# A causal mask moved from VectorE's maximum to TensorE, with a new written-out order of the first pass

## What is computed

```python
h = _ln(x, ln1_g, ln1_b)
qkv = h @ W_attn + b_attn
q, k, v = jnp.split(qkv, 3, axis=-1)
...
att = jnp.einsum('bhtd,bhsd->bhts', q, k) * scale
causal = jnp.tril(jnp.ones((T, T), bool))
att = jnp.where(causal[None, None], att, -jnp.inf)
att = jax.nn.softmax(att, axis=-1)
sa = _merge(jnp.einsum('bhts,bhsd->bhtd', att, v)) @ W_aproj + b_aproj
x = x + sa
```

## Time and profile before

| | |
|---|---|
| median of 3 runs | 4394.42 us |
| lowest and highest | 4390.21, 4397.11 us |
| the profiled execution | 4394.35 us |
| its span, first to last instruction | 4392.4 us |
| busy over the span: TensorE matmul, VectorE, ScalarE, GpSimd | 97%, 84%, 58%, 34% |
| matmuls | 33536 |
| mean granted TensorE clock | 0.987 |

### The profile page before, as it was taken

One profiled execution on the slowest core, in us unless ns is written; L12 is line 12 of the kernel. 1 busy time (PEld: TensorE's weight loads), 2 busy tenths in 40 slices (PEclk: granted clock), 3 DMA queues, 4 the chain that ended last, 5 costly groups with the idle time before them and its releaser, 6 DMA issues. The chain is left out here.

```text
span 4392.4 us, 98493 instructions
## 1 busy us (share of the span) xinstructions
PE 4270.3 (97%) x33536; PEld 3443.1 (78%) x33536; DVE 3687.5 (84%) x12709; ACT 2543.8 (58%) x6753; POOL 1481.0 (34%) x1941
## 2 busy tenths in 40 slices
PE   5999999999999899999999999999999999999998
PEld 4788888888887678777787878778888888888886
DVE  4899999999997899999999999967777777777774
ACT  2556565665655454545555454536676767676765
POOL 3344444444443233334333433331212121212121
PEclk7999999999999999999999999999999999999999
DMA  5455554545544454544545454433222222222220
GB/s 168 140 155 149 143 155 133 156 140 143 153 140 131 136 144 132 145 137 143 160 123 156 124 147 131 141 95 88 61 79 61 79 61 79 61 76 64 72 65 8
DMA packets 406436, 513.34 MB, mean 117 GB/s; under 512 B 133808, under 2 KB 373936, under 8 KB 384432
## 3 DMA queue, kind: packets, MB, share of 16 engines
q1 hardware_dynamic: 398544, 496.82, 39.7%
q10 hardware_dynamic: 7392, 10.24, 0.8%
HBM read 266.30 MB, written 236.72 MB: 115 GB/s over the span
## 5 line engine op out<-in xcount | busy, mean ns | idle before, releaser
L811 ACT ACTIVATE probs_own<-bank 128x384 f32<-128x384 f32 (+2 forms) x1280 | 640.9, 570 | 69.2 <-DVE bank L1060 40.9
L718 ACT ACTIVATE ht<-bank,columns_l 128x256 f32<-128x256 f32 x384 | 197.4, 571 | 718.2 <-PE bank L1237 715.9
L625 POOL TENSOR_SCALAR veps<-meanvar 128x2 f32<-128x2 f32 x256 | 65.1, 254 | 1403.9 <-DVE meanvar L961 1403.9
L1184 PE MATMUL bank<-ht,w_ff 128*128 128x256 f32 x2048 | 492.6, 384 | 2.7 <-ACT ht L718 1.6
L1184 PE MATMUL bank<-w_ff,ffh 128*128 128x256 f32 x2048 | 475.8, 381 | 0.2
L1041 DVE DVE_READ_ACCUMULATOR2_ANT nmf_own<- 128x1 f32 x3072 | 425.3, 138 | 0.0
L1184 PEld LDWEIGHTS bank<-w_ff,ffh 128*128 128x128 f32 x2048 | 379.0, 190 | 49.5 <-issue 1.2
L1041 DVE CUSTOM_DVE_ANT_0 bank<-bank,mask_rows 128x256 f32<-128x256 f32 x1024 | 398.1, 454 | 20.9 <-PE bank L1184 20.8
L1184 PEld LDWEIGHTS bank<-ht,w_ff 128*128 128x128 f32 x2048 | 371.2, 191 | 50.5 <-ACT ht L718 2.8
L1184 PE MATMUL bank<-kstack_own,qstack_own 96*128 96x256 bf16 (+2 forms) x3072 | 372.6, 249 | 27.8 <-DMA kstack_own<-k_parts 19.4
L876 ACT ACTIVATE probs_other<-bank,negmax 128x120 f32<-128x120 f32 x1024 | 356.6, 383 | 59.4 <-DVE negmax L1164 59.4
(11 more groups left out here) (164 smaller groups left out, 9946.0 us busy)
## 6 DMA issues: line engine op xcount, KB each, us to landing
qstack_own<-q_parts SPq DMA_DIRECT2D x96, 768.0 KB, 5.6
kstack_own<-k_parts SPq DMA_DIRECT2D x64, 768.0 KB, 7.5
qstack_other<-q_parts SPq DMA_DIRECT2D x64, 768.0 KB, 5.9
q_parts<-q_parts_own SPq DMA_DIRECT2D x96, 384.0 KB, 2.5
q_parts<-q_parts_own SPq DMA_DIRECT2D x96, 256.0 KB, 2.2
k_parts<-k_parts_own SPq DMA_DIRECT2D x64, 384.0 KB, 3.0
q_parts<-other_parts SPq DMA_DIRECT2D x64, 384.0 KB, 2.5
other_words<-k_parts SPq DMA_DIRECT2D x64, 360.0 KB, 3.3
```

The costliest lines, as they stand in the source:

```text
L625: nc.gpsimd.tensor_scalar(veps[key][:, :], meanvar[key][:, :, 1], r["norms"][key]["eps"], None, ALU.add).then_inc(veps_ready.sem, 1)
L718: return nc.scalar.activation(out, in_, ACT.Identity, scale=scale, bias=bias)
L811: nc.scalar.activation(probs[key][0:rows, j % a.slots, 0:n], bank_of(u)[0:rows, 0:n], ACT.Exp, scale=a.scale).then_inc(a_done.sem, 1)
L1184: return nc.tensor.matmul(out, lhsT, rhs, start=first, stop=True, skip_group_check=True)
```

## The change

Three things are edited.

1. The own attention of `l0` gets `max_on` "pe" in place of "dve". In each `scores_max.own` step TensorE adds the causal mask with one more matmul. For numbers 0 to 3 it covers 4 x 128 = 512 columns, for 4 to 11 the latter 128 keys of both heads, 2 x 128 = 256. VectorE takes the maxima with one plain reduction a step (12 an element) in place of 32 adding reductions.
2. `LISTS["l0"]` is new on all engines: other planned times and another order, of the same steps.
3. `START` and every pair of `SPREAD` are new, and with them the planned times of the weights' loads in `l1` and `l2`. The other steps of `l1` and `l2` keep their planned times.

```diff
-START = {"l0": 0.0, "l1": 33.12879, "l2": 66.18842}
+START = {"l0": 0.0, "l1": 32.18041, "l2": 65.42448}
...
         "PE": """
-            norm.0.0/0.24343 project_k.own.0/0.29714 project_q.own.0/0.33916 scores_max.own.2/0.81786 scores_max.own.8/0.82319
...
-            scores_max.own.10/1.03455 scores_max.own.11/1.07681 negate_t.own.0/1.16618 project_k.other.0/1.16900
-            project_v.own.0/1.20141 scores_exp.own.1/1.26914 scores_exp.own.6/1.27312 scores_exp.own.3/1.27715
...
-            probs_v.own.3/1.62892 project_out.own.0/1.73382 norm.1.0/2.06623 project_q.other.0/2.12416
-            scores_max.other.3/2.48486 scores_max.other.5/2.49010 scores_max.other.4/2.49534 scores_max.other.6/2.54260
...
-            probs_v.other.2/3.40602 probs_v.other.3/3.41650 project_out.other.0/3.64697 norm.2.0/3.92324 ff_in.ff.0/3.97118
...
-            ff_out.ff.3/4.88122
+            norm.0.0/0.38849 project_k.own.0/0.48748 project_q.own.0/0.53048 scores_max.own.5/0.92925 scores_max.own.9/0.93693
...
+            scores_max.own.1/1.05144 scores_max.own.2/1.06168 negate_t.own.0/1.15251 project_v.own.0/1.15520
+            scores_exp.own.2/1.23082 scores_exp.own.1/1.23968 scores_exp.own.4/1.24352 scores_exp.own.0/1.25238
...
+            project_out.own.0/1.57077 project_k.other.0/1.64178 norm.1.0/1.75792 project_q.other.0/1.80836
+            project_v.other.0/2.20564 scores_max.other.2/2.22579 scores_max.other.1/2.23466 scores_max.other.7/2.24736
...
+            probs_v.other.1/2.73556 probs_v.other.3/2.74564 project_out.other.0/2.84866 norm.2.0/3.19550 ff_in.ff.0/3.27660
...
+            ff_out.ff.3/4.11221
...
-            nm_rows.own.0/1.19224 spill_k.other.1/1.96943 spill_k.other.2/1.97962 spill_k.other.0/1.98981
-            spill_q.other.0/2.20243 spill_q.other.1/2.23654 spill_q.other.2/2.27011 stack_k.other.0/2.28030
-            stack_q.other.0/2.34355 nm_rows.other.0/2.75429 store.x.0/4.95924 loads.first.0/0.03 loads.rest.0/4.00
+            spill_q.own.1/0.64678 spill_q.own.2/0.67898 stack_k.own.0/0.69555 stack_q.own.0/0.77323 nm_rows.own.0/1.17051
+            load_c.c.0/1.19441 spill_q.other.0/1.88062 spill_k.other.1/1.92322 spill_k.other.0/1.93300 spill_k.other.2/1.96315
...
+            nm_rows.other.0/2.54579 store.x.0/4.18464 loads.first.0/0.03 loads.rest.0/4.00 loads.rest.1/4.25 loads.rest.2/4.50
...
-            ff_in.ff.0/4.44412 ff_in.ff.3/4.54045 weights.own_qkv.0/-0.86728 weights.own_o.0/-0.33458
-            weights.other_qkv.0/0.97570 weights.other_o.0/1.58128 weights.ff1.0/2.58060 weights.ff2.0/2.89333
+            ff_in.ff.0/4.44412 ff_in.ff.3/4.54045 weights.own_qkv.0/0.04015 weights.own_o.0/0.44884 weights.other_qkv.0/1.08632
+            weights.other_o.0/1.72709 weights.ff1.0/2.70276 weights.ff2.0/3.04690
...
     r["atts"] = {"own": Att("causal", (w_own[:, 0], bq0, "0"), (w_own[:, 1], bk0, "0"), (w_own[:, 2], None, "0"), w_own[:, 3], bv0, "causal",
-                            "dve", "pool"),
+                            "pe", "pool"),
```

More of the change, by code:

```diff
@@ new lines @@
+            scores_max.other.5/2.40366 negate_t.other.0/2.52778 scores_exp.other.4/2.61107 scores_exp.other.5/2.61619
+            scores_exp.other.3/2.62131 scores_exp.other.0/2.62643 scores_exp.other.7/2.63154 scores_exp.other.1/2.63666
+            scores_exp.other.6/2.66263 scores_exp.other.2/2.66774 probs_v.other.0/2.71537 probs_v.other.2/2.72544
+            probs_v.other.1/2.73556 probs_v.other.3/2.74564 project_out.other.0/2.84866 norm.2.0/3.19550 ff_in.ff.0/3.27660
+            ff_in.ff.1/3.41252 ff_in.ff.3/3.67286 ff_in.ff.2/3.76807 ff_out.ff.0/3.88895 ff_out.ff.1/3.96764 ff_out.ff.2/4.07191
@@ L85 @@
[L85 to L89, removed]
@@ new lines @@
+            scores_exp.own.10/1.38295 scores_exp.own.8/1.39158 scores_exp.own.13/1.40021 scores_exp.own.15/1.40885
+            scores_exp.own.14/1.41880 norm.1.0/1.77435 split_hi_k.other.0/1.81253 split_hi_q.other.0/1.85831
+            split_mid_q.other.0/1.90087 split_mid_k.other.0/1.91217 scores_exp.other.3/2.64178 scores_exp.other.0/2.65288
+            scores_exp.other.4/2.66398 scores_exp.other.1/2.67507 scores_exp.other.5/2.68617 scores_exp.other.6/2.69727
+            scores_exp.other.7/2.70837 scores_exp.other.2/2.71946 norm.2.0/3.21193 ff_in.ff.0/3.32318 ff_in.ff.1/3.45910
@@ L97 @@
[L97 to L106, removed]
@@ L107 @@
-            ff_mid.ff.2/4.74993 ff_mid.ff.3/4.80456 ff_out.ff.0/4.94017 masks.l1.0/1.2
+            stats.0.0/0.18045 norm.0.0/0.35289 split_rest_k.own.0/0.55637 split_rest_q.own.0/0.61023 scores_max.own.5/0.94321
+            scores_max.own.9/0.97120 scores_max.own.6/0.98511 scores_max.own.8/0.99902 scores_max.own.11/1.01294
+            scores_max.own.0/1.02685 scores_max.own.3/1.04076 scores_max.own.4/1.05467 scores_max.own.7/1.06859
+            scores_max.own.10/1.08250 scores_max.own.1/1.09641 scores_max.own.2/1.11033 negate.own.0/1.12691
@@ new lines @@
+            negate.own.1/1.13215 negate.own.2/1.13738 negate.own.3/1.14262 negate_t.own.0/1.16149 project_v.own.0/1.20464
+            probs_v.own.0/1.44130 probs_v.own.1/1.49155 heads_rec.own.0/1.50912 heads_mul.own.0/1.51819 heads_back.own.0/1.54160
+            project_out.own.0/1.64036 stats.1.0/1.66856 norm.1.0/1.73342 split_rest_k.other.0/1.85392
+            split_rest_q.other.0/1.88062 project_v.other.0/2.23207 scores_max.other.2/2.23998 scores_max.other.1/2.25315
+            scores_max.other.7/2.26632 scores_max.other.4/2.27949 scores_max.other.0/2.33972 scores_max.other.6/2.38325
@@ new lines @@
+            scores_max.other.5/2.41496 scores_max.other.3/2.42813 negate.other.0/2.45619 negate.other.1/2.46143
+            negate.other.2/2.47815 negate.other.3/2.51552 negate_t.other.0/2.53676 probs_v.other.0/2.75192
+            probs_v.other.1/2.76681 heads_rec.other.0/2.79587 heads_mul.other.0/2.80494 heads_back.other.0/2.82507
+            project_out.other.0/2.89668 stats.2.0/2.91348 norm.2.0/3.14518 ff_in.ff.0/3.46398 ff_in.ff.1/3.57243
+            ff_mid.ff.1/3.62629 ff_mid.ff.0/3.65448 ff_in.ff.3/3.78170 ff_mid.ff.3/3.83984 ff_in.ff.2/3.86331
@@ new lines @@
+            spill_q.own.1/0.64678 spill_q.own.2/0.67898 stack_k.own.0/0.69555 stack_q.own.0/0.77323 nm_rows.own.0/1.17051
+            load_c.c.0/1.19441 spill_q.other.0/1.88062 spill_k.other.1/1.92322 spill_k.other.0/1.93300 spill_k.other.2/1.96315
+            spill_q.other.1/1.97292 spill_q.other.2/1.99023 stack_k.other.0/2.02669 stack_q.other.0/2.06924
+            nm_rows.other.0/2.54579 store.x.0/4.18464 loads.first.0/0.03 loads.rest.0/4.00 loads.rest.1/4.25 loads.rest.2/4.50
+            loads.rest.3/4.75 loads.rest.4/5.00 loads.rest.5/5.25 loads.rest.6/5.50 loads.rest.7/5.75 loads.rest.8/6.00
@@ L125 @@
+            loads.rest.9/6.25 loads.rest.10/6.50 loads.rest.11/6.75 loads.rest.12/7.00
         """,
@@ L223 @@
             turn3.three.7/3.39381 turn3.three.5/3.40487 turn3.three.6/3.41593 turn3.three.4/3.60407 probs_v3.three.2/3.67373
-            probs_v3.three.3/3.72971 weights.own_qkv.0/-1.01656 weights.own_o.0/-0.14547 weights.q3.0/1.10377
-            weights.fc.0/2.49220 weights.k3.0/-18.0 weights.v3.0/-17.0
+            probs_v3.three.3/3.72971 weights.own_qkv.0/-1.20671 weights.own_o.0/-0.33700 weights.q3.0/0.91168
+            weights.fc.0/2.32588 weights.k3.0/-18.0 weights.v3.0/-17.0
         """,
```

51 lines of the change are left out of this document (21 added, 30 removed), and 6 rows, old and new, of the table SPREAD.

## The result

The changed kernel takes 4423.6 us in the median of four runs (4420.14 to 4426.79) against 4394.4: a ratio of 1.0069, with an interval of 1.0056 to 1.0081. It is slower by 29 us; the forecast was 4398, with a range up to 4431. The profiled execution took 4423.67 us.

A forecast was written before the change was run, and what follows sets the result against it. The prediction took TensorE's matmuls as the bound, VectorE close behind. Its terms, 0 at element 3, +35 for 28 periods, -34 and +3 for the handovers, gave +4 on 4394.35: 4398 us, range 4363 to 4431.

The forecast's parts named there:

- TensorE as the bound, price of the mask: First pass: TensorE sets the pace, so 12 more mask matmuls cost 1.74 us per element, their weight loads 0.
- Rival (d): TensorE is not the bound and the masks fit into gaps: period stays 42.66, total 4363 us; chance 0.03.
- Relief of VectorE: First pass's own maxima: plain reductions save VectorE 2.9 us per element, of which 0.5 comes back in TensorE's waits.
- rival (e): Own maxima: plain reductions relieve VectorE little, 9.2 us against 10.1, returning 0.2 us per element; total 4406; chance 0.04.
- rival (b): VectorE held more than its waits show: steady period 43.4, thin first periods 3 us shorter each, total 4375; chance 0.26.
- Element 0's transposes come 2.9 us earlier: Start of the first pass: transposes of element 0's own maxima at 44.8 us, not 47.7, through shorter maxima.
- The fill, 123 us: First pass, element 0 to 3: three thin periods of 38, 41 and 44 us, 123 together against 119.6 before.
- The handover, -34: First pass's element 31 to second pass's element 4: 5.20 units of 44.5 us plus 4, 235 against 269.0 us.
- The weights' wait: Head of the second pass: TensorE waits for newly loaded w_own and w_other, together 4 us.
- Third handover and end: Second to third pass and the last elements: +3 us for the third pass's later start, 0 for the end.
- the forecast's own case: Whole kernel: extra matmuls and the shorter handover between passes cancel, 4385 to 4412 us; chance 0.36.
- rival (c): First to second pass: handover does not shrink as queues wait, total 4429; decided if element 4 stands past 1648; chance 0.31.

The follow-up runs named there:

- x_first: The changed kernel with the first block of weight loads put behind the load of element 0's x in SyncE's queue; 4405.76 us, ratio 1.0031.
- x_late: The kernel before the change with the load of element 0's x put behind the first block of weight loads; 4409.06 us, ratio 1.0037.
- reduce_no_mask: The kernel before with the own maxima as plain reductions and their causal mask left out, old order kept; 4362.92 us, ratio 0.9935.
- l2_back: x_first with the third pass's start, pairs and weight loads set back to those of the kernel before; 4406.13 us, ratio 1.0033.
- mask_only: The kernel before, old order and starts, with only the mask of the own maxima moved to TensorE; 4409.44 us, ratio 1.0040.
- x_first_no_mask: x_first with the plain reductions kept and the causal mask of the maxima left out; 4402.95 us, ratio 1.0022.
- gap_back: x_first with the second pass's old distance from the first, the third keeping its new distance from the second; 4435.53 us, ratio 1.0096.

## Why the prediction came out as it did

*TensorE as the bound, price of the mask:* right. 1.74 us an element taken, 1.72 and 1.78 measured in the old order; 0.22 and 0.11 us for the two widths, as taken; weight loads at 0. Rival (d) is out. The new order with the mask has the same period, 43.65 against my 43.9.

*Relief of VectorE:* right in kind, small by 0.3 us. I took 0.5 a period, between 0 and 1.0; the runs give 0.80. The eleven reductions of 512 columns above took (6.66 - 0.69) / 10 = 0.60 each, as assumed, where 0.69 is how long one that stands alone lasts in the same timeline. So rival (e) is not borne out. The Trainium skill ("VectorE: DVE Perf Modes", section "Rules for kernel authors") calls this reduction the engine's slowest operation; this case does not bear that out, since going over to it took 3.5 us of VectorE's time off each element. The 28 periods gave +27.8 and not +35. The measured 43.65 lies midway between the forecast's 43.9 and rival (b)'s 43.4.

*"Element 0's transposes come 2.9 us earlier":* wrong, they came 13.8 later, and this is the largest error. The step that failed is the sentence on SyncE's queue, "not on any path, I think". I had compared the order of the steps in the list, and for SPREAD had used the pairs of the last element and of the second and third pass's first. The pair of the first pass's element 0 was left out, and it was the one in which the x load sits; x_first and x_late put it at 16 to 18 us. The 2.9 us of shorter maxima were there, 47.7 against 44.4 in reduce_no_mask, and element 0's own masks, which the sum had at nothing in the start, go against them: 46.3 with one mask a step, 47.3 with two, though these steps are hardly larger than the scatter named above.

*The fill, 123 us:* mis-sized, 130.1 measured and 128.8 without the late x. My "each holds more work" was worth 3.4 us in the sum; it is some 100 matmuls, 14 us. The other term, the shorter chain of maxima, was not sized apart, and it is larger than I allowed: in the old order the fill takes 119.6 us before and 113.1 with the plain reductions and no mask, at granted clocks of 0.82 and 0.84, so VectorE's relief gives 6 us there. With the masks it is 115.0 at 0.90, still shorter than before.

*The handover, -34:* the right sign, -26 measured. The weights' wait that I feared, 4 us of the sum, is not among the waits there: the three loads of `w_own` were issued from 1416.3 to 1417.3 us, the last landed 3.6 us after its issue (6.2 before), and TensorE's first use of them, at 1421.16, shows no wait. The 5.20 units, which I had at 44.5 us each, took 242.7 / 5.20 = 46.7, with 20.1 us idle where I expected 12. My account of the limit had 14 us of matmuls of the tail "done earlier" as a gain; it was 21 us of work. But work that leaves the stretch behind element 31's transposes enters the one ahead of element 3's: the sum booked it in full at the one end and hardly at the other. The 13.6 us by which x_first's span (4406.0) is longer than that of before are -1.0 up to element 0, +9.2 in the fill, +26.8 to element 31, -22.5 in the handover and +1.0 behind it.

*Third handover and end:* +3 taken, +3.7 measured, but l2_back shows that the new values there bring nothing that can be told from zero. In the changed kernel the last stretch was 102.3 us against 99.0 with the same 546 matmuls; the clock was 0.89 in it, 0.92 before. x_first, which has the same steps there, took 100.3 at 0.92.

The total of 4423.6 is 26 us above the forecast of 4398 and outside the 4385 to 4412 that I gave the forecast's own case. It lies inside the whole range, up to 4431, by luck: that end was set by rival (c), and (c)'s cause is not what happened, since the handover did shrink, while the largest cause, the late x, is in no rival. The point that I gave for it, the second pass's element 4 later than 1648, was passed (1656.4) through the 24 us of the start and the fill. A time from the start of the span collects every error ahead of it; the distance from element 31 would have told the cases apart. By the sign that I had set myself, element 4 off by more than 16 us, the account was wrong in kind: it was 24 us off. That holds for the start and the fill; the steady period did rise as forecast.

Put together, the 29 us are 16 to 18 for the late x load, 16 for the mask with its relief (mask_only's median; its profiled execution, 9 us above that median, has -1.4 up to element 0, -4.6 in the fill and +27.5 from there to element 31), and -4 for order and distances together, 4405.8 against 4409.4, which is within the spread of mask_only's own runs. So the new order and the shorter distance, with 21 us less in the handover and 14 more in the fill than mask_only has, come to nothing that these runs can tell from zero.

What stays open: whether the old order could take a shorter distance of the passes, and whether an order that lays other work both ahead of the transposes and behind them, as x_first_no_mask seems to need, would fall below 4362.9. No run has either.

## What to carry to other kernels

When a change reorders a pipeline, keep a ledger of TensorE's work between two recurring marks: what a new order takes from the tail it puts into the head, so look for the gain in the idle time that goes. Look up the new position of every step of the very first element, loads above all, since a shift that is harmless between neighbours can put the first input behind all weights. And price a cost in the order in which it will stand: the same masks were worth 1.75 us an element in the old order and 0.09 in the new, where TensorE waits for the maxima as long as the masks would have taken.

## What the runs showed that I had not expected

In the fill no cost of the masks can be seen. The windows from element 0's transposes to element 3's, with no mask and with two, beside mask_only's above:

```profile
44.40:157.50 113.10, 91.99 (x714) 69.36 (x715) 74.81 (x185) 48.77 (x115) 42.09 (x79) 0.84 0.50 140
```

```profile
47.30:160.60 113.30, 93.73 (x786) 70.96 (x787) 74.97 (x185) 49.05 (x115) 42.09 (x79) 0.92 0.50 140
```

With 714, 750 and 786 matmuls the stretch is 113.1, 115.0 and 113.3 us long and TensorE busy 92.0, 92.6 and 93.7, while the granted clock goes from 0.84 over 0.90 to 0.92 (0.90 to 0.92 is also the difference between x_first and gap_back, which have the same fill). At full clock the 72 matmuls between the first and the last are two masks for each of three elements, 2 x 3 x 1.74 = 10.4 us of work. Why the clock is higher with them was not tested.

The first x took 7.7 us from issue to first use behind the weights' transfers (16.11 to 23.85) and 3.0 us ahead of them (0.79 to 3.79): of the 20 us by which it came late 15.3 are the place in the queue and 4.7 the longer time to its use. That the weights' transfers still under way make up the latter is likely, but no run shows it by itself.
